# Where the group means of the first sign convolution come from, and in which order projection and convolution run over the images

## The reference

```python
def _L0_conv_ref(x, qkv_w, qkv_conv_w, conv5_w, conv7_w, conv9_w, proj_w, temperature, num_heads):
    kv = jnp.einsum('oc,bchw->bohw', qkv_w, x)
    kv = _dw3x3(kv, qkv_conv_w)              # depthwise 3x3, zero padded
    k, v = jnp.split(kv, 2, axis=1)
    q = _ssl(x, conv5_w, conv7_w, conv9_w)   # wavelets, depthwise 3x3, inverse wavelets
...
    attn = jax.nn.softmax(jnp.einsum('bhdn,bhen->bhde', q, k) * temperature, axis=-1)
    out = jnp.einsum('bhde,bhen->bhdn', attn, v).reshape(b, c, h, w)
    return jnp.einsum('oc,bchw->bohw', proj_w, out)

def _L1_conv_ref(x, w1, gamma1, beta1, w2, gamma2, beta2):
    identity = x
    out = ste_sign(x)
    out = conv3x3(out, bin_weight(w1))       # sign(w) * mean|w|
    out = batchnorm(out, gamma1, beta1)      # over all four images
    out = ste_sign(out)
    out = conv3x3(out, bin_weight(w2))
    out = batchnorm(out, gamma2, beta2)
    return out + identity
...
    x = x + _L0_conv_ref(_gn(x), ...)
    x = x + _L1_conv_ref(_gn(x), ...)
    return x
```

## Time and profile before

| | us |
|---|---|
| median of 3 runs (lowest, highest) | 1455.79 (1451.62, 1458.39) |
| the profiled execution | 1448.98 |
| its span, first to last instruction | 1447.1 |
| stage 4 begins | 981.18 |
| end of the first sign convolution | 1224.13 |
| the second sign convolution | 1231.92 to 1375.46 |

### The profile page before, as it was taken

How to read it: one execution, slowest core, us unless ns; L and a number is a source line. 1 busy time by engine, 2 the same in 40 slices (tenths; PEclk the granted TensorE clock), 3 DMA queues, 4 the chain that set the end, 5 groups by cost and what they waited for, 6 DMA issues and landing times. The chain is left out here.

```text
span 1447.1 us, 35967 instructions
## 1 busy us (share of the span) xinstructions
PE 1186.5 (82%) x12644; PEld 926.0 (64%) x12644; DVE 1087.4 (75%) x1899; ACT 806.6 (56%) x1414; POOL 232.0 (16%) x241
## 2 busy tenths in 40 slices
PE   0999937889899898998989999725999998999900
PEld 0555537789899898988989898603555554555500
DVE  6677428999999899998999999445767654063394
ACT  0677745667767576675667666110442443866383
POOL 6100011131131311313213221102000010000000
PEclk9999958999999899999999999867899999999955
DMA  9976962534444345444444442067877430000069
GB/s 327 419 303 267 305 144 71 138 88 123 132 100 123 108 112 137 104 115 116 108 129 116 111 127 71 22 233 240 277 254 252 134 136 0 0 1 0 1 267 401
DMA packets 148700, 221.22 MB, mean 153 GB/s; under 512 B 115624, under 2 KB 116788, under 8 KB 144192
## 3 DMA queue, kind: packets, MB, share of 16 engines
q1 hardware_dynamic: 137456, 152.26, 34.8%
q0 software_dynamic: 6480, 47.19, 8.5%
q10 hardware_dynamic: 4608, 19.67, 4.0%
HBM read 131.84 MB, written 87.20 MB: 151 GB/s over the span
## 5 line engine op out<-in xcount | busy, mean ns | idle before, releaser
L885 DVE SCALAR_TENSOR_TENSOR b_value_sum<-b_vin,b_vtaps,b_value_sum 128x576 f32<-128x576 f32 x448 | 361.5, 807 | 2.4 <-ACT b_value_sum L811 2.0
L1608 PE MATMUL b_conv_bank<-b_sign,wsign 128*128 (+1 forms) x1728 | 296.8, 329 | 10.3 <-ACT b_sign L1388 7.7
L1608 PEld LDWEIGHTS b_conv_bank<-b_sign,wsign 128*128 128x128 bf16 x1728 | 168.7, 98 | 141.2 <-issue 29.0
L927 PE MATMUL b_bank<-b_yh,b_tmh 96*96 96x200 f16 x768 | 198.4, 258 | 53.5 <-DVE b_feat L892 23.6
L839 ACT CAST b_feat<-b_bank 96x400 f16<-96x400 f32 x255 | 124.9, 490 | 191.4 <-PE b_bank L929 188.0
L927 PE MATMUL b_bank<-b_tkh,b_kt 96*96 96x100 f16 x1536 | 224.5, 211 | 2.5 <-DVE b_tml L908 2.3
L929 PE MATMUL b_bank<-b_tkh,b_kt 96*96 96x100 f16 x1536 | 223.5, 211 | 0.0
L928 PE MATMUL b_bank<-b_tkl,b_kt 96*96 96x100 f16 x1536 | 223.4, 211 | 0.0
L927 PEld LDWEIGHTS b_bank<-b_tkh,b_kt 96*96 96x96 f16 x1536 | 194.9, 127 | 5.0 <-DVE b_tml L908 2.5
L929 PEld LDWEIGHTS b_bank<-b_tkh,b_kt 96*96 96x96 f16 x1536 | 195.1, 127 | 0.0
L929 PE MATMUL b_bank<-b_yh,b_tml 96*96 96x200 f16 x768 | 194.2, 253 | 0.0
(11 more groups left out here) (210 smaller groups left out, 2314.2 us busy)
## 6 DMA issues: line engine op xcount, KB each, us to landing
b_vin<-value_projection_scratch SPq DMA_DIRECT2D x32, 686.0 KB, 5.5
value_projection_scratch<-b_vout ACTq DMA_DIRECT2D x24, 784.0 KB, 4.6
keys_scratch<-b_khl SPq DMA_DIRECT2D x24, 784.0 KB, 3.5
b_kt<-keys_scratch SPq DMA_DIRECT2D x128, 147.0 KB, 3.0
b_xraw<-in_x SPq DMA_DIRECT2D x128, 144.0 KB, 5.0
values_scratch<-b_vacc SPq DMA_DIRECT2D x32, 576.0 KB, 3.2
b_values<-values_scratch SPq DMA_DIRECT2D x48, 384.0 KB, 3.7
out<-xs SPq DMA_DIRECT2D x25, 576.0 KB, 6.8
```

The lines of the kernel that those rows point to most:

```text
L885: nc.vector.scalar_tensor_tensor(whole if t == 8 else part, src, vtaps[:, t:t + 1], part, ALU.mult, ALU.add).then_inc(s_tap, 1)
L927: nc.tensor.matmul(out, w_hi, m_hi, start=first, stop=False)
L1608: ins = nc.tensor.matmul(cbank[k % NBK][:, 0:CH].rearrange("p (r c) -> p r c", c=W), p["wsign"][nth // NIMG][:, t * C:(t + 1) * C], padded ...
```

## The change

The mean over an image of `x1` is a sum of two terms: the mean of `x`, known in stage 1, and `pa_t` times the mean of the convolved values. The mean of a depthwise 3x3 convolution with zero padding follows from nine sums of its input: the mean of the image, the sums of its first and last row and of its first and last column, and its four corners. In the changed kernel, stage 1 keeps the means of `x` (`xmean`), sums the borders of `x` on DVE while the last image runs, normalises and projects them with one matmul of 36 columns on PE (at chunk 46 of the last image), and mixes them with the taps into `vmean`. Stage 4 starts with four matmuls of one column, one add and the group matmul, for all images at once. `group_mean` per image is gone.

Then projection and convolution run as one stream: six chunks of image 0 are projected, and from there on each `sign_conv` of a chunk is followed by the `project` of the chunk six places later, over the seams too. ACT signs eight rows as soon as their `add_x` is done. The first three value slots and the group matrix are loaded in stage 3, on SP, ahead of its wait for the softmax.

```diff
@@ stage 1 @@
+            sp.dma_start(value_taps[:], d["value_taps_reversed"]).then_inc(s_w, 16)
...
-            dve.wait_ge(s_w, 7 * 16)
+            dve.wait_ge(s_w, 8 * 16)
...
                 dve.sem_inc(s_mean, 1)
+                wait(V.tensor_copy(p["xmean"][:, b:b + 1], mv[:, 0:1]))
...
+            def border_sums(b):
+
+                image = x[:, b, :].rearrange("p (r c) -> p r c", c=W)
+                wait(V.tensor_copy(border[:, b, 0:1], p["xmean"][:, b:b + 1]))
+                wait(V.tensor_reduce(border[:, b, 1:3], image[:, 0:H:H - 1, :], AX.X, ALU.add))
+                wait(V.tensor_reduce(border[:, b, 3:5], image[:, :, 0:W:W - 1].rearrange("p r c -> p c r"), AX.X, ALU.add))
+                wait(V.tensor_copy(border[:, b, 5:9].rearrange("p (a b) -> p a b", b=2), image[:, 0:H:H - 1, 0:W:W - 1]))
...
+                    elif n == 11:
+                        mix_taps()
+                    elif 12 <= n < 12 + NIMG:
+                        border_sums(n - 12)
+                    elif n == 12 + NIMG:
+                        normalise_border()
+            value_means()
...
+                    elif k == BORDER:
+                        pe.wait_ge(s_border, 1)
+                        nc.tensor.matmul(psum_s[:, BORDER_COLS], wv_t[:], border[:].rearrange("p b q -> p (b q)"),
+                                         start=True, stop=True).then_inc(s_vborder, 1)
@@ stage 3, SP @@
             sp.dma_start(p["xs"][:, 0, :], d["x_c"][:, 0, :]).then_inc(p["s_x0"], 16)
+            sp.dma_start(p["gmean"][:], d["group_mean"]).then_inc(p["s_gmean"], 16)
+            for k in range(VSLOTS):
+                sp.dma_start(p["vs"][:, k, :], d["values"][:, k * VP * CH:(k + 1) * VP * CH]).then_inc(p["s_v"][k], 16)
             sp.wait_ge(s_go, 2)
@@ stage 4, ACT @@
+            def x1_sign(b, r, k):
+
+                act.wait_ge(s_x1, r * RC + (b * NCH + k + 1 + NBK))
...
+            for k in range(1, RC, NR // ROWS):
+                x1_sign(0, 0, k)
             for b in range(NIMG):
                 with act.Fori(0, RND - 1) as r:
                     for k in range(RC):
                         copy(b, k, r)
...
+                        if k % (NR // ROWS):
+                            x1_sign(b, r + 1, k)
+                for k in range(RC):
+                    copy(b, NCH - RC + k)
+                    if b + 1 < NIMG and k % (NR // ROWS):
+                        x1_sign(b + 1, 0, k)
@@ stage 4, DVE @@
+            x1_means()
+            for k in range(RC):
+                add_x(0, 0, k)
+                x1_stats(0, 0, k)
+            for b in range(NIMG):
                 with dve.Fori(0, RND - 1) as r:
                     for k in range(RC):
...
+                        add_x(b, r + 1, k)
                         y_stats(b, r, k)
...
+                        x1_stats(b, r + 1, k)
+                x1_variance(b)
+                if b + 1 < NIMG:
+                    dve.wait_ge(s_x[b], RND * 16)
@@ stage 4, PE @@
+            for b in range(NIMG):
+                ins = nc.tensor.matmul(psum_g[0][:, b:b + 1], p["pa_t"][:, b * C:(b + 1) * C], p["vmean"][:, b:b + 1],
+                                       start=True, stop=True)
+            ins.then_inc(s_vm, 1)
+            group_means()
+            for k in range(RC):
+                project(0, 0, k)
+            for b in range(NIMG):
                 with pe.Fori(0, RND - 1) as r:
                     for k in range(RC):
                         sign_conv(b, r, k)
...
+                        project(b, r + 1, k)
                 for k in range(RC):
                     sign_conv(b, RND - 1, k)
...
+                    if b + 1 < NIMG:
+                        project(b + 1, 0, k)
```

More of the change, by code:

```diff
@@ L54 @@
 SLAB = NIMG * H // NG
+VP, VSLOTS = 2, 3
 GUARD = 1e-30
@@ L1301, in block_convolutions @@
         s_carry = sem("b4_wait_carrier")
-        X1_STATS = [NCH + b * 2 * NCH - (RC if b else 0) for b in range(NIMG)]
+        X1_STATS = [RC + (b * RND + RND - 1) * 2 * RC for b in range(NIMG)]
         pieces = [(2, NPC - 1)] + [(2, q) for q in range(NPC - 1)] + [(b, q) for b in (3, 0, 1) for q in range(NPC)]
@@ L1326, in _ @@
         def _(sp):
-            sp.dma_start(gmean[:], d["group_mean"]).then_inc(s_c, 16)
             def load(start, k):
                 sp.dma_start(vs[:, k, :], d["values"][:, start]).then_inc(s_v[k], 16)
-            for k in range(VSLOTS):
-                load(ds(k * VP * CH, VP * CH), k)
             with sp.Fori(1, NIMG * RND) as r:
@@ L1409, in _ @@
             act.wait_ge(s_ready, 1)
-            for r in range(NP):
-                x1_sign(0, r)
+            for k in range(1, RC, NR // ROWS):
+                x1_sign(0, 0, k)
             for b in range(NIMG):
@@ L1415, in _ @@
                         copy(b, k, r)
-                last = NCH - RC
-                for k in range(last, NCH):
-                    copy(b, k)
-                    if b + 1 < NIMG and k > last:
-                        if k == last + 1:
-                            act.wait_ge(s_ready, b + 2)
-                        for r in range(2 * (k - last - 1), 2 * (k - last)):
-                            x1_sign(b + 1, r)
-                if b + 1 < NIMG:
-                    for r in range(2 * (RC - 1), NP):
-                        x1_sign(b + 1, r)
+                        if k % (NR // ROWS):
[4 more added lines that the diff above has]
+                        x1_sign(b + 1, 0, k)
             root(1, col[:, 0, 4:5], col[:, 0, 3:4])
-            act.wait_ge(s_ready, NIMG + 1)
+            act.wait_ge(s_ready, 2)
             done = 0
@@ L1623, in _ @@
                         sign_conv(b, r, k)
-                        project(b + 1, r + 1, k)
+                        project(b, r + 1, k)
                 for k in range(RC):
                     sign_conv(b, RND - 1, k)
-                    if k == 1:
-                        group_mean(b + 1)
-            for nth in range(NIMG - 1, 2 * NIMG):
+                    if b + 1 < NIMG:
+                        project(b + 1, 0, k)
+            pe.wait_ge(s_gsum, 2)
+            nc.tensor.matmul(psum_g[1][:, 0:NIMG], gmean[:], var[:, 0, :], start=True, stop=True).then_inc(s_grp, 1)
+            for nth in range(NIMG, 2 * NIMG):
                 with pe.Fori(0, RND - 1) as r:
@@ L1678, in build @@
         p["xs"] = sb("xs", [C, 2, HW])
+        p["vs"] = sb("values", [C, VSLOTS, VP * CH])
+        p["gmean"] = sb("group_mean", [C, C])
         p["s_x0"] = ctx.enter_context(nc.semaphore("first_image_in"))
+        p["s_gmean"] = ctx.enter_context(nc.semaphore("group_mean_in"))
+        p["s_v"] = [ctx.enter_context(nc.semaphore(f"values_in{k}")) for k in range(VSLOTS)]
         block_attention(nc, d, p)
```

127 lines of the change are left out of this document (64 added, 63 removed).

## The result

The changed kernel's four runs have a median of 1421.2 us (1415.1 to 1423.73), the kernel before 1454.64 beside them: a ratio of **0.9765 (95% interval 0.9734 to 0.9796)**. Five later runs gave 1415.43 against 1452.56, 0.975 (0.9716 to 0.9784). The forecast was 1423, the range 1413 to 1437.

What follows compares the result with a forecast made beforehand. PE's own pace was taken to bound the middle of an image, with 39.6 us lost at stage 4's start and seams. Terms -34.3 + 1.3 = -33.0 took 1448.98 to 1416.0; plus 6.8 gave 1422.8, rounded 1423, range 1413 to 1437.

Steps and rivals of the forecast that it cites:

- The stream: Stage 4: 90 projection and convolution pairs at 2.118 us plus six convolutions, 199.5 us, ending at 1189.8 instead of 1224.13.
- Start of the stream: Start of stage 4: small matmuls, then twelve projection passes, eight slow and four fast; stream starts at 990.3 (990.2 to 991.4).
- second condition: Start of stage 4: ScalarE's first sign waits until POOL has cleared the sign buffer, 8.11 us, so it ends at 990.2.
- Stage 4 in sum: Stage 4 to the end of the first convolution: 34.3 us less than the kernel before.
- Stage 1: Stage 1: later weights, column copies, border sums and an added matmul cost 1.3 us more (0 to 2.5).
- Stage 3: Stage 3: four more transfers issued while SP waits for the softmax cost nothing, upper bound 4.7 us.
- The upper bounds of 4.7 and 1.7: Most us lost if stage 3's last `abd` waited for the early transfers (4.7), and at stage 4's first value reload (1.7).
- Images late: Rival, stage 4: POOL's 20 image transfers fall behind, stalling PE before image 3; 1441 us, half way 1432; chance 0.12.
- The clock stays low: Rival, stage 4: PE's clock stays low for half of the first 45 us, 9.0 us more, 1432; chance 0.05.
- it does not reach the end: Rival: something else ends the first convolution or the kernel, so the gain is lost; about 1453 us; chance 0.03.
- value slots: Rival, stage 4: each of 45 value reloads lands too late and stops PE; 1463 us or more; chance 0.03.
- The signs that I named: Profile checks: convolution 9 us into stage 4, 2.12 us pairs, no image wait, stage 1 near 190.6; wrong if stage 4 later.

Runs made afterwards that it cites:

- Experiment 3: Changed kernel with the seams between images in the old order, group means still known early; stage 4 to the end of the first convolution 212.39 us against 209.35.
- experiment 2: Changed kernel without stage 1's border work, value means set to zero; first key chunk to last store of values 138.97 us against 141.38.
- 5: Changed kernel with GpSimd clearing only the border of the sign buffer; stage 4 to the end of the first convolution 209.14 us against 209.35.
- experiment 6: Changed kernel with nine unused matmuls on PE before its last wait of stage 3; stage 4 to the end of the first convolution 208.92 us against 209.35.
- after: First profile of the changed kernel, nothing else altered; stage 4 to the end of the first convolution 209.35 us against 242.95 in the kernel before.
- after again: Second profile of the unaltered changed kernel; stage 4 to the end of the first convolution 209.17 us, first key chunk to last store of values 142.93.
- 7: Changed kernel with stage 1's border work spread over the last image; first key chunk to last store of values 139.65 us against 141.38.
- experiment 1: Changed kernel with group matrix and first three value slots loaded at stage 4's start again; stage 4 to the first convolution's end 211.15 us against 209.35.
- experiment 8: Changed kernel with border work spread, only the sign buffer's border cleared, and unused matmuls (eleven and one) in stage 3's gaps; median 1413.07 us, second six runs 1413.05.
- 4: Changed kernel with two more transfers in GpSimd's chain ahead of image 3's loads; stage 4 to the end of the first convolution 209.27 us against 209.35.

## Why the prediction was right, point by point

- *The stream*: right. 90 pairs at 2.118 us and six convolutions, PE without a pause over the seams. Experiment 3 shows that both halves of the change count at a seam, the known means for some 3 us and the order for 1.
- *Start of the stream*, forecast 9.1 us after the start of the stage, measured 9.85. The mis-sized term is the clock in the twelve passes: I let it rise after eight (4.9 + 1.3), and they took 6.94, near the bound of all slow. The four matmuls were 1.85 for 2.1. That the second condition, the clearing of the sign buffer, falls at nearly the same place was right (experiments 2, 5 and 6).
- *Stage 4 in sum*, forecast -34.3: -33.6 in the first pair of profiles, -33.2 on average (209.1 in the four profiles in which nothing from stage 3 on was altered, after, after again, 2 and 7, against 242.3 in the two of before).
- *Stage 1*, forecast +1.3 with a bound of 2.5: 2.5 to 4.2 (experiment 2). This step failed. I put 0.4 us on four border sums between four key chunks; they cost PE two waits of 0.91, and in four of eight profiles the clock behind them, 1.7. Spread out, the same work costs some 0.5 (mean of the three profiles 139.27 against 138.76 in the three without it). VectorE's share of busy time, on which I relied, says nothing of four chunks in a row. The 0.6 us that I put on the weights and the copies ahead of the first key chunk is not settled: the chunk came 1.4 us later on average in the twelve profiles (40.9 against 39.5), by an effect that experiment 2 does not separate from scatter.
- *Stage 3*: nothing beyond the scatter, as forecast; the values are in time, and late ones cost 1.8 (experiment 1). The upper bounds of 4.7 and 1.7 did not come.
- *Images late*: the rival was close. I gave 4 us to spare; VectorE did wait 1.58 us in the profile after (in none of the nine others with the chain of 20 transfers), PE did not, and by the threshold of 157 us the spare was 157 - 154.3 = 2.7 there. The pace scatters: the last load was issued 138 to 147 us after the start. The Trainium skill, "DMA: Bandwidth & Descriptors", section on queues, rings and completion order, has the transfer engines take turns between queues; this case agrees in direction, with little of it: in the first convolution a load of a piece of an image took 6.8 us (median) in both profiles of the changed kernel against 6.3 and 5.7 before, a load of values 3.7 and 3.6 against 3.5 and 3.6.
- *The clock stays low*, *it does not reach the end*, *value slots*: none came; clock 1.00 in the stream, the copy follows the last convolution at once, PE waits for no reload.
- *The signs that I named*: the stream, its end and the clock came as said. Three did not: stage 1 ends 3.9 us later, not within 2.5; VectorE's first add of image 3 waits 1.58 us; and stage 4 starts 9.3 us later (990.48 against 981.18), which I had called a sign of being wrong. 3.9 of that is stage 1, 5.4 the scatter of stage 2.

The sum of the stages is about -29.7 (stage 4 -33.2, keys to store some +3.5, the rest scatter or not settled); the medians differ by 33.4 and 37.1. Part of that is that the two profiled executions of the kernel before (1448.98, 1445.84) lie below its median, as the prediction allowed for with 6.8; what remains is within the scatter of stage 2, and no run here settles it. So the mechanism and its size in stage 4 were right, but that 1423 lies within 2 us of 1421.2 is partly luck: the stages gave 3 us less than the -33.0 forecast.

## What to carry to other kernels

A statistic that follows from the input by algebra can be moved to a stage where its engine has room, and the gain is the wait that it ended, read from the chain at each place where it stood. But work put into the gaps of a nearly full engine must be laid out by the gaps, one piece to each: the same operations cost 2.5 to 4.2 us in a row and some 0.5 apart. Where a producer on another queue becomes just fast enough, work out the instant from which it costs, and expect its scatter to decide.

## What the runs showed of the hardware that was not expected

- What short stops of PE did to its clock: in experiment 6 the granted clock was 1.00 before and 0.50 after two stops of 1.97 and 1.11 us, and 0.80 again in the third stretch of stage 4; with both filled it stayed at 1.00 (experiment 8). Two stops of 0.91 us in stage 1 lowered it in four of eight executions of the same code (to 0.66 over 5 us in the second profile of the changed kernel) and not in the others.
- Operations of one column on VectorE, 0.16 us elsewhere, took up to 1.39 us in stage 1 while GpSimd worked on the taps. VectorE and GpSimd of the changed kernel, timelines:

```profile
30.61 0.59 DVE L359 TENSOR_TENSOR b_col<-b_mv,b_col 128x1 f32<-128x1 f32 x1
31.23 0.16 DVE L360 TENSOR_TENSOR b_col<-b_col 128x1 f32<-128x1 f32 x1
31.43 1.39 DVE L361 TENSOR_TENSOR b_col<-b_col,b_mv 128x1 f32<-128x1 f32 x1
...
34.18 1.24 DVE L373 SCALAR_TENSOR_TENSOR b_col<-b_col 128x1 f32<-128x1 f32 x1
```

```profile
30.27 0.91 POOL L280 TENSOR_TENSOR kparts<-kraw,khi 126x384 f16<-126x384 f32 x1
31.26 1.54 POOL L275 TENSOR_TENSOR qraw<-qraw,qscale 126x768 f32<-126x768 f32 x1
...
33.78 1.64 POOL L277 TENSOR_TENSOR qraw<-qraw,qhi 126x768 f32<-126x768 f32 x1
```

Each long one ends with GpSimd's operation: 31.20 and 31.18, 32.82 and 32.80, 35.42 and 35.42. The Trainium skill, "SBUF — State Buffer", section "SBUF: two separate sides", says that GpSimd and VectorE, the latter for operations with two inputs in SBUF among others, share one pair of ports, and that whichever starts first holds it for its whole instruction; these rows agree. From VectorE's first work to the first key chunk it takes 28.2 to 28.6 us in the nine profiles in which two of these operations take 1.39 and 1.24 us, and 26.6 to 27.0 in the five in which they do not (both of before, 3, 4 and 6). All nine are of the changed kernel or a variant; with two profiles of before, the runs do not say whether the change makes the later start more likely.
